# Moving the adds of a reduction tree from VectorE to GpSimd inside a selective scan

## The reference

```python
x = x + _layernorm(attn(_layernorm(x)))
x = x + _layernorm(ffn(_layernorm(x)))
# attn
xz = inputs @ W_in;  x, z = split(xz, 2)
x = silu(causal_conv4(x, conv_w) + conv_b)
x_dbl = x @ W_x;  dt_in, B, C = split(x_dbl, [1024, 1040])
dt = softplus(dt_in @ W_dt + b_dt);  A = -exp(A_log)
# per position t, channel i, state s
h[i,s] = exp(dt[t,i] * A[i,s]) * h[i,s] + dt[t,i] * B[t,s] * x[t,i]
y[t,i] = sum_s h[i,s] * C[t,s] + x[t,i]
return (y * silu(z)) @ W_out
# ffn: idx = argmax(log_softmax(logits) + gumbel(u));  x @ W[idx] + b[idx]
```

## Time and profile before

| | |
|---|---|
| median of 3 runs | 5392.52 us (5391.46 to 5398.43) |
| the profiled execution, its own time | 5395.03 us |
| its span on the slowest core (core 1) | 5393.1 us |
| spans of the 8 cores | 5263.0 to 5393.1 us |
| busy: PE, DVE, ACT, POOL | 32%, 56%, 19%, 2% of the span |
| scan stage (first `w_dt` load to the last states) | from 1551 us to about 4570 us |

### The profile page before, as it was taken

One profiled execution on the slowest core, in us unless ns is written; L12 is line 12 of the kernel. 1 busy time (PEld: TensorE's weight loads), 2 busy tenths in 40 slices (PEclk: granted clock), 3 DMA queues, 4 the chain that ended last, 5 costly groups with the idle time before them and its releaser, 6 DMA issues.

```text
span 5393.1 us, 21300 instructions; the slowest of 8 cores (5263.0 to 5393.1 us)
## 1 busy us (share of the span) xinstructions
PE 1750.2 (32%) x3461; PEld 351.2 (7%) x3461; DVE 2993.7 (56%) x3194; ACT 1034.8 (19%) x1454; POOL 124.9 (2%) x230
## 2 busy tenths in 40 slices
PE   1566667887330101010100221010101000566664
PEld 0111111111000000000000000000000000011110
DVE  4211111000028888888889158888888888233434
ACT  2111111000122222222222222222222221000000
POOL 0000001000100000000000000000000000000000
PEclk9778775555555555555555555555555555555555
DMA  2222323000200000000000000000000000100000
GB/s 60 45 63 61 63 61 73 0 0 1 40 10 8 16 12 12 14 10 14 8 12 2 10 10 16 8 16 8 16 8 16 6 12 27 67 24 24 24 16 27
DMA packets 55171, 123.78 MB, mean 23 GB/s; under 512 B 8574, under 2 KB 8702, under 8 KB 54918
## 3 DMA queue, kind: packets, MB, share of 16 engines
q0 software_dynamic: 25376, 44.35, 5.2%
q1 hardware_dynamic: 29670, 78.08, 4.2%
HBM read 128.73 MB, written 35.91 MB: 31 GB/s over the span
## 4 chain that ended last, share of the span: by engine, by line
DVE 52%; PE 25%; issue 11%; DMA 5%; ACT 5%; DVEq 1%; SPq 0%; POOL 0%; ACTq 0%; POOLq 0%
DVE big_b L679 11%; DVE big_b L665 11%; DVE big_b L687 6%; DVE sm L658 6%; PE psA L433 4%; PE psB L433 3%; PE psB L842 3%; PE psA L842 3%; PE psB L501 3%; PE psA L501 3%; DVE bigf L715 2%; DVE bigf L459 2%; DVE big_b L701 2%; DVE big_b L706 2%; DVE big_b L695 2%
## 5 line engine op out<-in xcount | busy, mean ns | idle before, releaser
L652 ACT ACTIVATE bigf<-bigf,pa 128x1024 f32<-128x1024 f32 x512 | 584.1, 1146 | 1628.4 <-DVE big_b L679 813.9
L598 PE MATMUL psB<-arena,big_b 128*128 128x512 bf16 x256 | 149.7, 585 | 2056.4 <-ACT bigf L612 2021.5
L679 DVE TENSOR_TENSOR_SCAN big_b<-bigf,hcol,sm 128x1024 bf16<-128x1024 f32 x256 | 601.9, 2351 | 45.4 <-DVE sm L658 45.1
L665 DVE TENSOR_TENSOR_SCAN big_b<-bigf,sm 128x1024 bf16<-128x1024 f32 x256 | 586.6, 2292 | 45.4 <-DVE sm L658 45.0
L607 DVE TENSOR_SCALAR bigf<-psB,bdtcol 128x512 f32<-128x512 f32 x32 | 23.9, 746 | 817.6 <-PE psB L598 817.6
L687 DVE TENSOR_TENSOR big_b<-big_b,big_a 128x1024 bf16<-128x1024 bf16 x512 | 351.8, 687 | 27.0 <-issue 0.2
L658 DVE TENSOR_TENSOR sm<-sm,big_a 128x1024 bf16<-128x1024 bf16 x512 | 350.5, 685 | 0.0
L454 DVE TENSOR_SCALAR bigf<-bigf,wcol 128x2048 f32<-128x2048 f32 x16 | 21.0, 1311 | 582.6 <-ACT bigf L441 582.6
L433 PE MATMUL psA<-arena,big_b 128*128 128x512 bf16 x512 | 247.2, 483 | 158.7 <-ACT sm L447 91.3
L433 PE MATMUL psB<-arena,big_b 128*128 128x512 bf16 x512 | 242.2, 473 | 66.8
L560 PE MATMUL psC<-big_b 1*128 1x512 bf16 x128 | 74.1, 579 | 489.0 <-DVE big_b L725 245.3
(11 more groups left out here) (126 smaller groups left out, 2055.1 us busy)
## 6 DMA issues: line engine op xcount, KB each, us to landing
sm<-ffn_w POOLq DMA_DIRECT2D x64, 256.0 KB, 6.7
bigf<-x SPq DMA_DIRECT2D x32, 512.0 KB, 3.8
big_b<-w_in POOLq DMA_DIRECT2D x32, 256.0 KB, 5.2
d_xconv<-big_a SPq DMA_DIRECT2D x16, 512.0 KB, 2.7
d_sz<-sm SPq DMA_DIRECT2D x16, 512.0 KB, 5.2
sm<-d_xconv SPq DMA_DIRECT2D x32, 256.0 KB, 2.9
sm<-d_sz SPq DMA_DIRECT2D x32, 256.0 KB, 3.2
big_b<-w_dt POOLq DMA_DIRECT2D x32, 256.0 KB, 3.8
```

Of the source, the lines that this page charges most:

```text
L598: return e.matmul(ps[:, 0:512], big_b[:, WDTn + par * 1024 + dp * 128:WDTn + par * 1024 + dp * 128 + 128], arena[:, dp * L + half * HF + l ...
L652: return e.activation(bigf[:, T1 + sp * 1024:T1 + (sp + 1) * 1024], bigf[:, DTB:DTB + 1024], AF.Exp, scale=pa[:, 256 + it * 16 + s:256 + i ...
L665: return e.tensor_tensor_scan(big_b[:, HLn:HLn + 1024], bigf[:, T1 + sp * 1024:T1 + (sp + 1) * 1024], sm[:, (6 + sp) * 1024:(7 + sp) * 102 ...
L679: return e.tensor_tensor_scan(big_b[:, HLn:HLn + 1024], bigf[:, T1 + sp * 1024:T1 + (sp + 1) * 1024], sm[:, (6 + sp) * 1024:(7 + sp) * 102 ...
```

## The change

The three bf16 adds of the tree (L695, L701, L706) are recorded for POOL in place of DVE. Their operands, buffers and places in the program order stay as they are. The add or the copy behind them (L711, L715) stays on DVE.

```diff
@@ -695,18 +695,18 @@
                         return e.tensor_add(big_b[:, L2n:L2n + 1024],
                                             big_b[:, L0n:L0n + 1024],
                                             big_b[:, L1n:L1n + 1024])
-                    kb.op("vector", f_pair, r=[LK[0], LK[1]], w=[LK[2]])
+                    kb.op("gpsimd", f_pair, r=[LK[0], LK[1]], w=[LK[2]])
                 if s % 4 == 3:
                     def f_pair1(e):
                         return e.tensor_add(big_b[:, L0n:L0n + 1024],
                                             big_b[:, L0n:L0n + 1024],
                                             big_b[:, L1n:L1n + 1024])
-                    kb.op("vector", f_pair1, r=[LK[0], LK[1]], w=[LK[0]])
+                    kb.op("gpsimd", f_pair1, r=[LK[0], LK[1]], w=[LK[0]])
                     def f_quad(e):
                         return e.tensor_add(big_b[:, L0n:L0n + 1024],
                                             big_b[:, L2n:L2n + 1024],
                                             big_b[:, L0n:L0n + 1024])
-                    kb.op("vector", f_quad, r=[LK[2], LK[0]], w=[LK[0]])
+                    kb.op("gpsimd", f_quad, r=[LK[2], LK[0]], w=[LK[0]])
```

## The result

The changed kernel takes 6084.4 us (median of 8 runs, 6081.34 to 6088.45; a ninth on record took 6092.78) against 5393.2 us of the kernel before in the same set. The ratio is 1.1277, 95% interval 1.1264 to 1.1289: 691 us slower. The forecast was 6255, its range 5840 to 6390. The direction, the three mechanisms and their order hold; the likeliest case's own range (from 6130) was missed on the low side, since each of the terms was priced somewhat too high. At 6084 the time also lies nearer to the first rival's 5973 than to the forecast's 6255, so the time alone does not tell the two apart.

A forecast was written before the change was run, and what follows sets the result against it. The prediction took DVE's row in the scan stage to bound the kernel. Adds costing 648 us (5.06 a group, 128 groups) and late loads costing 214 summed to 862, giving 6255 us, range 5840 to 6390.

The forecast's parts named there:

- the three mechanisms: Scan stage: uncovered fourth-state adds (+3.64 us a group), second-state add taking turns with DVE (+1.42), late weight load (7.65 a tile).
- the likeliest case: Second state's add on POOL and DVE take turns: 6255 us, own range 6130 to 6390, chance 52%.
- the first rival: Second state's add (L695) runs beside DVE: +2.84 us a group, 5973 us in all; chance 33%.
- DVE's row is the path: Scan stage: DVE works 1044.20 of 1200 us, so time leaving its row leaves the total unless new waits replace it.
- L701 and L706 have no cover: Fourth state: DVE's other work queues behind L715, so nothing hides these adds; 5.33 us for 1.69, +3.64 a group.
- X: Duration of one add on POOL, taken as 2.29 us from the L665 row, with bounds 0.69 and 2.35.
- L695 and DVE take turns: Second state's add on POOL delays L665 by 2.22 us; net of 0.80 saved, +1.42 us a group.
- The load: L578's weight load, issued after a tile's last L706, delays L607 and the second bank: 7.65 us a tile, 214 us.
- Beside each other: Second state's add on POOL overlaps DVE's work without holding it: 5973 us, down to 5910 with short handoffs; chance 33%.
- quick add: POOL's adds take 0.69 us beside DVE, but the loads still cost 214 us: 5560 to 5840 us; chance 6%.
- load costs nothing: PE gets its weights in time at the tile's end, so the 214 us go: 6043 us; chance 4%.
- faster: POOL adds at 0.69 us beside DVE and the load out of the way: -46 us, 5349 us; chance 2%.

The follow-up runs named there:

- quad_only: Against the kernel before, only L701 and L706 move to POOL and L695 stays on DVE: 5985.5 us, ratio 1.1099.
- pair_only: Against the kernel before, only L695 moves to POOL; L701 and L706 stay on DVE: 5505.6 us, ratio 1.0210.
- early_load: The changed kernel with each tile's weight load recorded ahead of the adds of the tile two before: 5875.8 us, ratio 1.0898 to the kernel before.

## Why the prediction was right, step by step

| term | predicted | in the changed kernel | where it is read |
|---|---|---|---|
| the two adds of the fourth state, a group | +3.64 us | 4.62 - 1.69 = +2.93 | wait at L715 |
| the add of the second state, a group | +1.42 | 5.02 - 3.33 - 0.80 = +0.89 | L658 to L687 |
| groups, x 128 | 648 us | 489 us | |
| load behind the adds, a tile | 7.65 | 5.72 + 1.52 = 7.24 | L607, and L607 to L658 |
| tiles, x 28 | 214 us | 203 us | |
| sum | 862 | 692 (measured 691) | |

- *DVE's row is the path.* Right. The changed kernel's tile takes 112.0 us (the d_yg stores at 2238.19 and 2686.02 are four tiles apart) where the one before took 89.2 (2287.78 to 2644.51, four tiles too): 22.8 more, against 4 x 3.82 + 7.24 = 22.5 from the table.
- *L701 and L706 have no cover.* Right, shown by quad_only. Mis-sized: X is 2.11 us and not 2.29, which is 128 x 2 x 0.18 = 46 us, and the three handoffs take 0.39 us (4.62 - 2 x 2.113) and not 0.75, another 46. The 0.51 us that I had averaged in is that of a DMA issue behind PE, and it does not hold for an add behind an add. The prediction's reason for 2.29 (that POOL would have to be far off DVE's best pass) speaks against the value rather than for it; that POOL's add came within 0.18 us of the scan's row was luck.
- *L695 and DVE take turns.* Right, shown by pair_only. No row of the trace before told it, and the prediction called it the weakest choice of its working. It decides the sign of the move of L695: with an add that runs beside DVE, pair_only would have been at 5291. Mis-sized by 0.53 us a group, 68 us in all. I let the add start when L658 ends; it starts 0.23 us after L658 does, and its last 0.14 us do not hold the scan. The rule of the Trainium skill (the page "SBUF — State Buffer", section "Who interferes with whom") agrees with every pair that was tried: a POOL instruction that reads holds a DVE instruction with two SBUF inputs (by 1.66 us), POOL's write alone does not (the scan keeps 2.29), and a DVE sum with one input is not held (1.21 us). That section calls the shared ports "an exclusive lock"; the trace differs at the edge, where the last 0.14 us of a 2.43 us add no longer hold the scan.
- *The load.* Right in place and size, shown by early_load (209 us against 214 forecast and 203 in the table). DVE's wait is 5.72 us in place of 6.13: the issue starts 0.05 us before the recorded end of L706 where 0.25 behind it was assumed, and from issue to L607 it takes 9.76 us where 9.93 was.
- *The price from a page.* The estimate of 2.25 us from the page "GPSIMD Engine Reference" of the Trainium skill (section "Performance versus the Vector engine") was nearer to the 2.113 measured for bf16 than my row of 2.29; both are above it.
- *The rivals.* "Beside each other" (33%) is refuted by pair_only and by the scan's 3.95 us; "quick add" by 2113 ns; "load costs nothing" by early_load; "faster" fell with both.

The range (5840 to 6390) held the time, but it was wide enough to hold the first rival's 5973 too, and the range of the likeliest case alone (from 6130) did not hold it. The terms all erred to the same side. For the length of an add (2.29, from rows of 0.69 to 2.35) and for the hold of L695 (the whole add, against none) the value had been taken at or near the upper end; the handoff (0.25, from 0.10 and 0.51) was below the middle of its rows and still too long.

## What to carry to other kernels

An engine that is 2% busy is not free help: ask first what the moved instruction will run beside. Here the test is whether POOL's instruction reads SBUF and whether DVE's reads two tensors from it. Then ask what stands behind the moved instructions in the helper's own row (here a load that cost 209 us), and what follows the result (here a wait of 4.62 us for 1.69 of work). The adds and the running sum on PE, which sums in PSUM and was busy for 110 of 1200 us in this stage, gave 8.0%.

## What was not expected of the hardware

- An add of two 128 x 1024 bf16 tensors takes 2.11 us on POOL and 0.69 on DVE, a ratio of 3.05; a POOL fill of the same size takes 0.95 us.
- An instruction that waits for its turn is shown as busy and long (3.95 in place of 2.29, 3.92 in place of 2.11), not as idle. The means by line hide it further: 2705 ns, since only one scan in four is held.
- From the recorded end of one instruction to the start of the one that waits for it lie 0.14 us from DVE to POOL, 0.15 from a POOL add to the next and 0.11 from POOL to DVE; a DMA issue behind a POOL add starts 0.05 us before the add's recorded end.
